# Four queues reordered around slot 0 of a token-routed expert layer

## The reference

```python
x = x + tanh(g_xattn[0]) * (fake_quant(layernorm(x)) @ fake_quant(ctx))   # 8-bit quantised operands
h = layernorm(x)
logits = h @ W_gate + b_gate                       # 8 experts
_, top_idx = top_k(logits, 2)
y_all = relu(einsum('bsd,edh->bseh', h, W_e) + b_e)
x = x + tanh(g_ffn[0]) * mean of y_all over the two chosen experts
```

## Time and profile before

| | |
|---|---|
| median of 3 runs | 336.47 us (336.21 to 336.8) |
| the profiled execution: time | 337.47 us |
| the profiled execution: span of the trace | 335.7 us |
| TensorE busy | 307.9 us (92%) |
| VectorE busy | 242.4 us (72%) |
| ScalarE busy | 146.6 us (44%) |
| GpSimd busy | 184.1 us (55%) |
| DMA | 81.49 MB, mean 243 GB/s |
| chain that ended last | TensorE 63%, VectorE 15%, GpSimd 5%, DMA 5%, issue 4%, ScalarE 4% |

### The profile page before, as it was taken

How to read it: one execution, slowest core, us unless ns; L and a number is a source line. 1 busy time by engine, 2 the same in 40 slices (tenths; PEclk the granted TensorE clock), 3 DMA queues, 4 the chain that set the end, 5 groups by cost and what they waited for, 6 DMA issues and landing times.

```text
span 335.7 us, 6287 instructions
## 1 busy us (share of the span) xinstructions
PE 307.9 (92%) x1601; PEld 233.3 (69%) x1602; DVE 242.4 (72%) x347; ACT 146.6 (44%) x147; POOL 184.1 (55%) x167
## 2 busy tenths in 40 slices
PE   4688999999979999999999999999999999999930
PEld 1233444786867888887888888888888888888820
DVE  2869999988798688599889576963559646963530
ACT  3769898945451911475447017410155006410110
POOL 5647535201002687687777557866548754876430
PEclk9999999979995999999999999999999999999985
DMA  6999945797674289899999978996449974365323
GB/s 215 414 409 386 401 184 170 272 379 256 242 267 174 80 275 327 203 278 349 402 355 338 385 209 193 328 343 174 79 132 340 298 198 110 93 137 113 60 81 62
DMA packets 19918, 81.49 MB, mean 243 GB/s; under 512 B 4160, under 2 KB 4160, under 8 KB 15808
## 3 DMA queue, kind: packets, MB, share of 16 engines
q1 hardware_dynamic: 12560, 58.76, 46.4%
q0 software_dynamic: 7200, 22.55, 29.1%
q10 hardware_dynamic: 144, 0.01, 0.0%
HBM read 62.43 MB, written 18.87 MB: 242 GB/s over the span
## 4 chain that ended last, share of the span: by engine, by line
PE 63%; DVE 15%; POOL 5%; DMA 5%; issue 4%; ACT 4%; DVEq 1%; ACTq 0%; SPq 0%; POOLq 0%
PE ps L1462 50%; POOL y_rows L510 4%; PE ps L1185 3%; PE ps_y L1214 3%; DVE w_lo L967 2%; DMA y_rows<-y_scratch,gidx 2%; DVE st L784 2%; PE ps_q L1242 2%; DMA stage<-in_ctx_dram 2%; PE ps_s L1238 2%; PE ps L1306 2%; DVE xt L840 2%; ACT u8c L569 1%; PE ps L1318 1%; POOL out_dram L532 1%
## 5 line engine op out<-in xcount | busy, mean ns | idle before, releaser
L510 POOL DMA_INDIRECT y_rows<-y_scratch,gidx x84 | 112.9, 1344 | 32.7 <-issue 25.0
L1462 PE MATMUL ps<-w_hi,yT_hi 128*128 x288 | 88.8, 389 | 0.8 <-DVE w_lo L967 0.8
L1462 PE MATMUL ps<-w_hi,yT_lo 128*128 x288 | 88.7, 389 | 0.0
L1462 PE MATMUL ps<-w_lo,yT_hi 128*128 x288 | 88.6, 389 | 0.0
L967 DVE TENSOR_TENSOR w_lo<-stage,w_hi 128x2048 f32 (+1 forms) x32 | 72.3, 2281 | 5.5 <-ACT w_hi L707 5.1
L698 ACT ACTIVATE yT_hi<-ps_y 128x1024 fp32r<-128x1024 f32 x21 | 21.6, 1027 | 123.7 <-PE ps L1462 69.3
L1462 PEld LDWEIGHTS ps<-w_hi,yT_hi 128*128 128x128 f32 x288 | 53.9, 188 | 12.5 <-issue 1.2
L1462 PEld LDWEIGHTS ps<-w_hi,yT_lo 128*128 128x128 f32 x288 | 54.1, 188 | 11.2
L1462 PEld LDWEIGHTS ps<-w_lo,yT_hi 128*128 128x128 f32 x288 | 54.1, 188 | 11.2
L532 POOL DMA_INDIRECT out_dram<-res,sidx x20 | 33.4, 1672 | 45.2 <-DVE res L1101 32.1
L707 ACT ACTIVATE w_hi<-stage 128x2048 f32 (+1 forms) x28 | 51.9, 1908 | 14.3 <-DMA stage<-in_L_ffn_W_e_dram 9.2
(11 more groups left out here) (200 smaller groups left out, 297.1 us busy)
## 6 DMA issues: line engine op xcount, KB each, us to landing
stage<-in_L_ffn_W_e_dram SPq DMA_DIRECT2D x32, 1024.0 KB
stage<-in_ctx_dram SPq DMA_DIRECT2D x16, 512.0 KB, 11.3
xt<-in_x_dram SPq DMA_DIRECT2D x8, 512.0 KB, 11.1
y_scratch<-y SPq DMA_DIRECT2D x8, 512.0 KB, 5.9
out_dram<-xt SPq DMA_DIRECT2D x8, 512.0 KB, 4.4
bias<-in_L_ffn_b_e_dram SPq DMA_DIRECT2D x8, 512.0 KB, 5.2
y_rows<-y_scratch,gidx POOLq DMA_INDIRECT x84
out_dram<-res,sidx POOLq DMA_INDIRECT x20
```

Source lines behind the costliest of these rows:

```text
L510: pool.indirect_dma_start(out=y_rows[q][:, b * QD:(b + 1) * QD], out_offset=None, in_=y_quarters[:, :], in_offset=bass.IndirectOffsetOnAxi ...
L1462: last = pe.matmul(ps[q][:, h * 512:(h + 1) * 512], lhs[q][:, k, :], w[:, bass.ds(woff + k * D + h * 512, 512)], start=(k == 0 and lhs is ...
```

## The change

On GpSimd the scatter of slot 0 now comes ahead of the gather for slot 3. ScalarE copies the last tile's logits, between bringing slot 0 into order and its high part; VectorE's copy in `select` is gone. On VectorE the low part of chunk 3 of expert 0 is made before `select(1)` and no longer between `sign(1)` and `positions(1)`; the transpose of slot 2's rows comes one weight split earlier; bias and weighing of slot 1 come ahead of the transpose of slot 3's rows and of the last split. On TensorE `place_second` moves ahead of the last of the eight pieces of the high-by-high product, the wait for the fourth low chunk takes the place of the wait for the third, and the high-by-low product is cut 3, 2, 2, 1 in place of 2, 2, 2, 1, 1. Slot 0's high part is still copied in one piece.

```diff
--- before.py
+++ after.py
@@ -533,10 +533,10 @@
                                         out_offset=bass.IndirectOffsetOnAxis(ap=sidx[:, q:q + 1], axis=0),
                                         in_=res[q][:, :], in_offset=None, compute_op=ALU.add).then_inc(s_sc, 16)

+            pool.wait_ge(s_post, 1)
+            scatter(0)
             pool.wait_ge(s_gi, 2)
             gather(1)
-            pool.wait_ge(s_post, 1)
-            scatter(0)
             pool.wait_ge(s_gi, 3)
             gather(0)
             pool.wait_ge(s_sc, 16)
@@ -717,6 +717,7 @@

             act.wait_ge(s_first, 16)
             put_in_order(0, res[0])
+            keep_logits(NT - 1, NT)
             evacuate_hi(0, yE_hi)
             for i in range(TPB, NT):
                 add_rowsum(i)
@@ -857,9 +858,6 @@
                 if g == 0:
                     dve.wait_ge(s_gate, e)
                 else:
-                    dve.wait_ge(s_gate, e)
-                    dve.wait_ge(s_gc, 1)
-                    dve.tensor_copy(logits_T[:, NT - 1 - TPB, :], ps_g[0:E, (NT - 1 - TPB) * P:(NT - TPB) * P]).then_inc(s_gc, 1)
                     dve.wait_ge(s_lgt, g)
                 dve.tensor_tensor(u(lg), gates_in[g][:, 0:n * E].rearrange("p (i e) -> p i e", e=E),
                                   bg.unsqueeze(1).to_broadcast([P, n, E]), ALU.add).then_inc(s_lg, 1)
@@ -1030,9 +1028,9 @@
                 make_onehot(i)
             split_lo(2, 3, slice(2 * CW, 3 * CW))
             read_rowsums(1)
+            split_lo(3, 4, slice(3 * CW, 4 * CW))
             select(1)
             sign(1)
-            split_lo(3, 4, slice(3 * CW, 4 * CW))
             positions(1)
             first_onehot(1)
             slot_matrix(1)
@@ -1110,17 +1108,17 @@
             dve.wait_ge(s_free, 3)
             weigh(0, fl(W0))
             split_lo1(0)
+            turn_rows(0, 1)
             split_lo1(1)
-            turn_rows(0, 1)
             evacuate_lo(2, yT_lo[0])
             split_lo1(2)
-            dve.wait_ge(s_el, 3)
-            turn_rows(1, 1)
-            split_lo1(3)
             dve.wait_ge(s_mm, 2)
             add_bias(1, 0)
             dve.wait_ge(s_free, 4)
             weigh(1, fl(W1))
+            dve.wait_ge(s_el, 3)
+            turn_rows(1, 1)
+            split_lo1(3)
             evacuate_lo(3, yT_lo[1])

             def step(slot, q, turn):
@@ -1419,17 +1417,16 @@
             pe.wait_ge(s_eh, 1)
             products(0, yE_hi, w_hi, 0, 2)
             counts(1)
-            products(0, yE_hi, w_hi, 2, KT)
+            products(0, yE_hi, w_hi, 2, 7)
             place_second()
+            products(0, yE_hi, w_hi, 7, KT)
             place_rows(0, 2, TPB)
-            pe.wait_ge(s_lo, 3)
-            products(0, yE_hi, w_lo, 0, 2)
+            pe.wait_ge(s_lo, 4)
+            products(0, yE_hi, w_lo, 0, 3)
             place_rows(1, 4, 6)
-            products(0, yE_hi, w_lo, 2, 4)
+            products(0, yE_hi, w_lo, 3, 5)
             place_rows(1, 6, NT)
-            products(0, yE_hi, w_lo, 4, 6)
-            pe.wait_ge(s_lo, 4)
-            products(0, yE_hi, w_lo, 6, 7)
+            products(0, yE_hi, w_lo, 5, 7)
             pe.wait_ge(s_abs, 1)
             for b in range(NQ):
                 last = pe.matmul(ps_r[:, b * E * SPE:(b + 1) * E * SPE], spread[:, b, :], tok_abs[:, :], start=True, stop=True)
```

## The result

The changed kernel takes 339.2 us (median of 17 runs, 337.52 to 341.89) against 336.55 for the kernel before (17 runs, 336.01 to 342.08); the ratio is 1.0074, with a 95% interval of 1.0053 to 1.0094. It is slower. The forecast was 332.4, the range 331.5 to 335.2, and "slower" had a chance of 0.05. The profiled execution took 338.79 with a span of 337.0, 1.3 more than before. Three executions among the experiments lasted 403.78, 455.4 and 625.03 us, far above all others; the ratios are formed without them, the medians with them.

The account below looks back on a forecast made before the run. TensorE, busy without a break from 155.83 us, was taken as the bound, so an earlier slot 1 moves the end: -3.8 - 0.8 + 0.5 = -4.1, giving 333.4 profiled and 332.4 as median, range 331.5 to 335.2.

Parts of the forecast that it names:

- the old wait in slot 4: TensorE's 0.8 us wait for a `w_lo` part goes if slot 4's rows land by 132.3: -0.8 us.
- new waits: What slots 3 and 4 may wait anew on TensorE: +0.5 us, bounds 0 and 3.2.
- POOL: GpSimd queue: scatter(0) takes 1.64 us after a 0.9 wait, gather(1) runs 115.4 to 122.1, slot 4's rows land at 132.3.
- The lock: VectorE splits fully blocking GpSimd's gather parts for 2.3 us each would make the sum -1.1; rejected from the row at 117.51.
- The landing and slot 3: Slot 3's rows land 125 to 128 and need 4.9 us more, ready 130 to 133; slot 3 due at 131.9.
- Split and logits moved: Chunk 3's split fills VectorE's idle time, 88.5 to 90.7, and ScalarE copies the logits for 0.3 us: cost nothing.
- selection to slot matrix: positions(1) starts at 94.55 instead of 96.17, `R` ends at 96.6, place_second starts at 96.8: TensorE's gap is gone.
- slot 0 on TensorE: `qidx` ends at 106.85, 2.45 us earlier, and slot 1 starts at 110.2 instead of 114.06.
- Term one: Slot 1's earlier start on TensorE: -3.8 us, or -1.1 if the low clock lasted 10.2 us again.
- The slow rival: Slot 4's rows land after 136.9 because scatter(0) waits longer ahead of gather(1): at 138, +1.1, 337.6 us; chance 0.05.
- VectorE's new order around the results: Slot 1's bias and weighing ahead of turn_rows(1) and the last split: expert 1's `w_lo` at 129.5, needed at 131.9, free.

Follow-up runs that it names:

- experiment 1: Changed kernel with gather(1) ahead of scatter(0) again on GpSimd, all else as changed: ratio 1.0004 to the kernel before, median 337.55 us.
- experiment 5: Changed kernel with gather(1) ahead of scatter(0), and VectorE turning slot 2's rows and making their low part before three weight splits: ratio 0.9934, 334.79 us.
- experiment 11: Changed kernel with the last split of expert 1 ahead of the turn of slot 3's rows on VectorE: ratio 1.0117, 340.83 us.
- experiment 7: Changed kernel with SP beginning expert 2's loads only when slot 3's rows have landed: ratio 1.0103, 341.22 us.
- experiment 2: Kernel before with only GpSimd's order changed, scatter(0) ahead of gather(1): ratio 1.0091, 340.43 us.
- experiment 8: Kernel before with only the logits' copy on ScalarE and the moved split of chunk 3: ratio 0.9962, 335.98 us.
- experiment 3: Changed kernel with GpSimd's order and VectorE's order around the results of slots 0 and 1 as before: ratio 0.9984, median 336.19 us.
- experiment 6: Changed kernel, scatter(0) still first, with VectorE turning slot 2's rows and making their low part before the weight splits: ratio 0.9974, 336.67 us.
- experiment 10: The changed kernel itself timed again, beside the kernel before on one chip: ratio 1.0059, 339.11 us.
- experiment 4: Changed kernel with SP's loads of expert 2 held back until the low part of slot 2's rows is made: ratio 1.0081, 339.77 us.
- experiment 9: The kernel of experiment 5 with slot 4's gather also ahead of scatter(0) on GpSimd: ratio 1.0228, 345.72 us.

## Why the prediction was wrong

The sum forecast -4.1 for the profiled execution: -3.8 for slot 1's start, -0.8 for the old wait in slot 4, +0.5 for new waits. The trace has -3.25, -0.8 and +3.54, and +1.7 for a spell at 1.2 GHz that no term had: +1.2, and the span grew by 1.3.

- **POOL, the step that failed.** "gather(1) runs 115.4 to 122.1, with its 6.7 us of now": it ran 117.96 to 126.15, 8.2, and so ended 4.0 late. It began 2.6 late: slot 0's weighing ended 0.5 later (113.94 for 113.4); the scatter began 0.9 after that end, a step that my sum put at nothing; and the scatter, priced at 1.64, took 2.85. The other 1.5 us are the parts' durations. They were carried over from the old order, although the change moves the splits that set them: two parts took 2.41 and 2.97.
- **The lock, weighed and turned down.** First the rows: every part that began beside a split ended 0.8 to 0.9 us after its end, in the old trace too: 117.51 + 1.90 = 119.4, where the first of the two splits from 116.31 had ended at 118.5. I read that part against the end of the second split and took it for a mere slowdown. It was held by the first and went through between the two. Its neighbours in GpSimd's timeline of the kernel before, which I had not read against the splits, say the same:

```profile
...
116.19 1.02 POOL L510 DMA_INDIRECT y_rows<-y_scratch,gidx  x1 [0.30 <-issue]
...
119.71 1.89 POOL L510 DMA_INDIRECT y_rows<-y_scratch,gidx  x1 [0.30 <-issue]
...
```

  The first began 0.12 ahead of the split and was not held; the second ended 0.8 after the second split's end (120.8). The Trainium skill (SBUF, "Who interferes with whom") says that a VectorE instruction with two SBUF inputs and a GpSimd one that reads SBUF exclude each other; by that rule a part that begins beside a split is held to its end, and the trace agrees, here and in experiments 1, 5 and 11. These rows do not show an exclusion in the other direction: the parts begun at 116.19 and let through at 118.5 ran on beside a split, and the two splits kept their time (4.47). My own sum by the rule was -1.1: nearer, but still of the wrong sign, for it left out that the scatter is held too, and had no spell at 1.2 GHz.
- **The landing and slot 3.** I had slot 3's rows land between 125 and 128, that is 2.9 to 5.9 us after the last part. The lag was 5.2, within that; 125 to 128 moved by the 4.0 of the step above is 129 to 132, and the turn came at 131.3. Experiment 7 shows that the loads of expert 2 are 3.3 us of the lag. The sum also had `yT_lo` of slot 3 at 130 to 133, past the 131.9 at which slot 3 was due, and gave that little weight. Slot 3 then waited 3.54, where I had +0.5 for slots 3 and 4 together and 3.2 as its upper bound. In slot 4 no wait was left, as forecast.
- **Split and logits moved; selection to slot matrix; slot 0 on TensorE** ("Term one: -3.8"): right as a chain, each time within 0.1 us up to `qidx`; slot 1 came 0.6 later than forecast (110.8 for 110.2), as ScalarE took slot 1's rows at 106.19 and only then the picks. But the base was an execution with 10 us at 1.2 GHz. Experiment 2 shows the same slot 0 with the gap and without the spell: slot 1 at 111.62. Against that the front is worth 0.8 us, not 3.3. The forecast took the whole -3.8 from the median as well, though about half the executions behind such a median have no low clock to win back (14 of 27 in experiment 8). The fastest order tried, experiment 5, is 0.7% under the kernel before, 2.4 us, and not 4.
- **The slow rival** had the right mechanism (scatter(0) with its wait ahead of gather(1)) and the wrong place and price: it decided at slot 3, and brought a spell at 1.2 GHz of 1.7 us that no term of mine had. The 0.05 was too low because its "against", a POOL wait of 0.9, counted the wait (it was 1.97) and not what the scatter and the splits do to the four parts behind it.
- **VectorE's new order around the results, costed at "free"**: it puts a split each at 113.9, 117.2 and 120.5, with other work between, so that each holds another operation of GpSimd. Experiments 1 and 3 put 3.4 us on it at the end of gather(1); experiments 5 and 6 show that another order makes the whole faster.

## What to carry to other kernels

When an engine's order changes, the durations of its neighbours change with it: reprice each operation that will now start beside what was moved, instead of carrying its old duration along. Ask of every gather when its last part leaves the queue and what traffic it meets then, for each slot that comes after, not only for the one that waits now. And look for a low clock in the one profiled execution before counting its removal as a gain: a second profile, or the mean granted clock of each timed execution, tells how often it comes.

## What the runs showed of the hardware

- An indirect gather's part that takes 0.95 us on GpSimd takes 1.3 to 3.0 when it begins beside a 128x2048 float32 subtraction of two SBUF tiles on VectorE: it ends 0.8 to 0.9 us after the subtraction, however late in it it began (1.3 in experiment 2, begun 0.4 before that end; 3.0 in experiment 1); VectorE's instruction keeps its 2.28. Back to back, two or three such subtractions let one part through at each boundary (1.86 to 1.90). An indirect scatter held in this way took 2.85 in place of 1.64.
- After waits of 3.5 and 3.7 us ahead of slot 3 the granted clock was 0.50 for 3.4 us (the changed kernel, experiment 10); around waits of 3.5, 4.1 and 4.8 us it was 0.50 for 6.8 to 6.9 us, beginning inside the wait (experiments 2, 4 and 11). After 0.9, 1.3 and 1.5 us it stayed at 1.00 (experiments 1, 3, 6), after 2.4 us in experiment 7 it was 0.50 for 3.4. But 1.0 us with short matmuls behind it was followed by 10.2 us at 0.50 in one profile and by none in another (experiment 2).
- The rows of a gather were turned 1.8 us after its last part with no loads under way (experiment 7), 5.2 with three 1 MB loads started from 116.3 to 123.0 (the changed kernel), and 5.0 to 5.9 in the kernel before and experiments 1 and 4.
- An indirect accumulating scatter issued at 129.29, with three 1 MB loads started from 123.9 on and a fourth at 133.6, let the operation that waited for its landing begin at 140.33 (experiment 9).
